# A graph layer on one core: the dense edge counts in rows of nine tiles instead of groups of four

## What is computed

```python
src = h[edge_src]
parts = [relu(h)]
for t in range(3):
    msg = relu(src @ W_e[t].T + b_e[t])
    msg = where((edge_type == t)[:, None], msg, 0)
    parts.append(segment_sum(msg, edge_dst, num_segments=6250))
agg = concatenate(parts, axis=1)                  # 6250 x 512
for t in range(3):
    o = agg @ W_n[t].T + b_n[t]
    updated = where((node_type == t)[:, None], o, updated)
return x + (updated + h)
```

## Time and profile before

| | |
|---|---|
| median of 3 runs | 1460.96 us (1460.74 to 1462.85) |
| the profiled execution | 1458.84 us, its span 1456.6 us |
| PE busy | 1417.5 us (97%) |
| DVE busy | 1086.0 us (75%) |
| POOL busy | 1003.6 us (69%) |
| ACT busy | 565.4 us (39%) |
| mean granted clock of PE | 0.987 of 2.4 GHz |

### The profile page before, as it was taken

How to read it: one execution, slowest core, us unless ns; L and a number is a source line. 1 busy time by engine, 2 the same in 40 slices (tenths; PEclk the granted TensorE clock), 3 DMA queues, 4 the chain that set the end, 5 groups by cost and what they waited for, 6 DMA issues and landing times.

```text
span 1456.6 us, 29052 instructions
## 1 busy us (share of the span) xinstructions
PE 1417.5 (97%) x10079; PEld 1180.2 (81%) x10079; DVE 1086.0 (75%) x3644; ACT 565.4 (39%) x1099; POOL 1003.6 (69%) x1065
## 2 busy tenths in 40 slices
PE   7969999999999999999999999999999999999997
PEld 3447888888888888888888888888888888888874
DVE  5888887877887778878777878777766777677632
ACT  5755444344444334434434434334323333323310
POOL 2347777777777777777777777777777777777760
PEclk9989999999999999999999999999999999999998
DMA  8562322322332262323222322432222222222220
GB/s 280 181 190 73 85 77 71 90 76 65 89 90 78 57 200 69 89 68 88 67 72 75 85 70 75 132 108 57 58 66 63 68 62 61 58 73 62 62 54 25
DMA packets 95629, 126.32 MB, mean 87 GB/s; under 512 B 21135, under 2 KB 72838, under 8 KB 95484
## 3 DMA queue, kind: packets, MB, share of 16 engines
q0 software_dynamic: 32384, 66.39, 18.0%
q1 hardware_dynamic: 62222, 57.05, 12.2%
q10 hardware_dynamic: 878, 1.02, 0.2%
HBM read 98.69 MB, written 25.68 MB: 85 GB/s over the span
## 4 chain that ended last, share of the span: by engine, by line
PE 92%; DVE 4%; issue 1%; DMA 1%; ACT 1%; POOL 0%; DVEq 0%; SPq 0%; ACTq 0%; POOLq 0%
PE ps L684 41%; PE ps L668 25%; PE ps L654 14%; PE ps L703 7%; PE ps L701 3%; PE ps L591 1%; PE ps L700 1%; DMA message_table<-work 1%; PE ps L691 1%; DVE arena L1059 1%; DVE work L1150 0%; DVE lhot L1061 0%; PE ps L589 0%; DMA work<-message_table 0%; DVE acc L1125 0%
## 5 line engine op out<-in xcount | busy, mean ns | idle before, releaser
L531 POOL DMA_INDIRECT rows<-message_table,idx x1012 | 980.1, 968 | 359.6 <-issue 279.0
L829 ACT CAST arena<-ps 128x500 f16<-128x500 f32 x900 | 473.9, 579 | 779.1 <-PE ps L668 768.9
L684 PE MATMUL ps<-mem,arena 128*120 128x384 bf16 x3675 | 681.1, 328 | 1.5 <-DVE mem L1155 1.5
L684 PEld LDWEIGHTS ps<-mem,arena 128*120 128x120 f16 x3675 | 480.2, 135 | 90.1 <-issue 4.4
L1059 DVE TENSOR_SCALAR arena<-iota_j,jkey 128x400 bf16<-128x400 f16 (+2 forms) x1800 | 492.4, 334 | 79.8 <-PE ps L668 77.6
L668 PE MATMUL ps<-arena,lhot 128*128 128x200 bf16 (+2 forms) x3600 | 441.0, 272 | 10.4 <-DVE lhot L1061 6.7
L668 PEld LDWEIGHTS ps<-arena,lhot 128*128 128x128 bf16 x3600 | 353.8, 105 | 56.3 <-DVE lhot L1061 7.9
L1125 DVE TENSOR_TENSOR acc<-ps,acc 128x20 f32 (+1 forms) x703 | 134.2, 191 | 239.8 <-PE ps L654 154.0
L1061 DVE TENSOR_TENSOR lhot<-ps,lkey 128x512 bf16<-128x512 f32 x448 | 303.4, 677 | 0.0
L654 PEld LDWEIGHTS ps<-onehot,rows 128*128 128x128 f32 x2024 | 254.5, 194 | 10.8 <-issue 6.5
L654 PE MATMUL ps<-onehot,rows 128*128 128x27 f32 x2024 | 249.0, 263 | 5.6 <-DVE acc L1125 5.6
(11 more groups left out here) (107 smaller groups left out, 330.5 us busy)
## 6 DMA issues: line engine op xcount, KB each, us to landing
rows<-message_table,idx POOLq DMA_INDIRECT x1012
message_table<-work SPq DMA_DIRECT2D x49, 192.0 KB, 2.0
work<-message_table SPq DMA_DIRECT2D x21, 448.0 KB, 4.4
kept_planes<-work SPq DMA_DIRECT2D x14, 672.0 KB, 3.2
mem<-kept_planes SPq DMA_DIRECT2D x14, 672.0 KB, 4.7
own_hT<-work SPq DMA_DIRECT2D x49, 64.0 KB, 1.7
work<-own_hT SPq DMA_DIRECT2D x49, 64.0 KB
xr<-in_x_dram SPq DMA_DIRECT2D x48, 64.0 KB, 2.1
```

The costliest lines, as they stand in the source:

```text
L531: pool.indirect_dma_start(out=rows[:, g % SLOTS, u, :], out_offset=None, in_=table_rows, in_offset=bass.IndirectOffsetOnAxis(ap=idx[:, g, ...
L684: m = pe.matmul(psQ[q % 2][0:BG * WG, 0:3 * D], counts[q % 2][:, c * MC + e, :], planes[:, c * MC + e, :, :].rearrange("p v d -> p (v d)") ...
L829: act.copy(counts[q % 2][:, half * HH:(half + 1) * HH, k * WG:(k + 1) * WG], psB[m % 3][:, 0:HH * WG].rearrange("p (h w) -> p h w", w=WG)) ...
```

## The change

The last 79,274 edges (79,488 places) are cut into 69 *wide rows* of nine tiles (1152 edges) instead of 150 groups of four. A wide row has 40 slots, with offsets `D_OFF` and widths `D_WID` (sum 72) for its nine tiles; three wide rows make a batch (again 120 columns in a product), 23 batches, 69 with the three types. The gathered groups are 248. There are 49 values of h in place of 50.

A build is now half a wide row: side 0 has the hots of tiles 0 to 4, side 1 of tiles 5 to 8; tile 4 reaches over the middle and has buffers of its own. A build has two parts of ten slots each, all 49 values of h in one bank (490 columns), and a tile that crosses a border of ten slots is multiplied in two pieces: 3, 4, 4 and 3 matmuls for the four parts, 14 a wide row. The column hot is laid out with the slot outside and h inside, and the matmul's output is the same PSUM layout as before (h outside, here ten slots inside) but written in the order of the hot. ACT copies a part of 490 to ten columns of `counts`. One iota serves all widths. The edge list needs 12 loads for 16. DVE's preparation works on two arrays of 512 and one of 1152 per partition. DVE adds three times 40 slots per batch. DVE waits for the last turned keys before the second build's hots, where it waited before the fourth's.

```diff
-BATCHES = 25
-BG = 6
+BATCHES = 23
+BW = 3
+BG = 2 * BW
+WT = 9
+WE = WT * P
...
-LEFT = 12
 WG = 20
-HB = 50
-HH = HB // 2
+D_OFF = (0, 3, 8, 11, 16, 21, 24, 27, 31)
+D_WID = (9, 9, 8, 8, 7, 6, 7, 9, 9)
+D_WS = 9
+D_MID = 21
+D_AT = 5
+MT = 4
+SL = 40
+PC = 10
+OWN = ((0, 1, 2, 3), (5, 6, 7, 8))
+LEFT = 24
+HB = 49
...
+            def hots(i, u):
+                if u == MT:
+                    return lmid[:, i // 2 % 2, :], jmid[:, i // 2 % 2, :]
+                return lhot[:, i % HOTS, OWN[i % 2].index(u), :], jhot[:, i % HOTS, JAT[u]:JAT[u] + HB * D_WID[u]]
+
             def count(i):
                 pe.wait_ge(dhot_ok, i + 1)
-                for half in range(2):
-                    m = 2 * i + half
+                for part in range(2):
+                    m = 2 * i + part
                     if m >= 3:
                         pe.wait_ge(d_count, m - 2)
-                    to = psB[m % 3][:, 0:HH * WG].rearrange("p (h w) -> p h w", w=WG)
-                    for u in range(TPG):
-                        a = JAT[u] + half * HH * WID[u]
-                        t = pe.matmul(to[:, :, OFF[u]:OFF[u] + WID[u]], lhot[:, i % HOTS, u, 0:P],
-                                      jhot[:, i % HOTS, a:a + HH * WID[u]],
-                                      start=(u == 0), stop=(u == TPG - 1), skip_group_check=True)
+                    low = (2 * (i % 2) + part) * PC
+                    tiles = [u for u in range(WT) if D_OFF[u] < low + PC and D_OFF[u] + D_WID[u] > low]
+                    to = psB[m % 3][:, 0:HB * PC].rearrange("p (h w) -> p w h", w=PC)
+                    for u in tiles:
+                        a, z = max(D_OFF[u], low), min(D_OFF[u] + D_WID[u], low + PC)
+                        rows_hot, cols_hot = hots(i, u)
+                        t = pe.matmul(to[:, a - low:z - low, :], rows_hot,
+                                      cols_hot[:, HB * (a - D_OFF[u]):HB * (z - D_OFF[u])],
+                                      start=(u == tiles[0]), stop=(u == tiles[-1]), skip_group_check=True)
                     t.then_inc(d_build, 1)
...
-                    act.copy(counts[q % 2][:, half * HH:(half + 1) * HH, k * WG:(k + 1) * WG],
-                             psB[m % 3][:, 0:HH * WG].rearrange("p (h w) -> p h w", w=WG)).then_inc(d_count, 1)
+                    act.copy(counts[q % 2][:, :, a:a + PC],
+                             psB[m % 3][:, 0:HB * PC].rearrange("p (h w) -> p h w", w=PC)).then_inc(d_count, 1)
...
-                for u in range(TPG):
-                    w = WID[u]
-                    dve.tensor_scalar(jhot[:, i % HOTS, JAT[u]:JAT[u] + HB * w], iota_j[w][:, :],
-                                      float(t * HB * w), jkey[:, g, u:u + 1], ALU.add, ALU.is_equal)
-                dve.tensor_tensor(lhot[:, i % HOTS, :, :], (iota_l[:, :] if i < 2 else iota_n).unsqueeze(1).to_broadcast([P, TPG, P]),
-                                  lkey[:, g, :].unsqueeze(2).to_broadcast([P, TPG, P]), ALU.is_equal).then_inc(dhot_ok, 1)
+
+                def column_hot(to, u):
+                    dve.tensor_scalar(to, iota_j[:, 0:HB * D_WID[u]], float(t * JT), jkey[:, w, u:u + 1],
+                                      ALU.add, ALU.is_equal)
+
+                numbers = iota_l[:, :] if i < 2 else iota_n
+                for u in OWN[side]:
+                    column_hot(jhot[:, i % HOTS, JAT[u]:JAT[u] + HB * D_WID[u]], u)
+                if side == 0:
+                    column_hot(jmid[:, i // 2 % 2, :], MT)
+                    dve.tensor_tensor(lmid[:, i // 2 % 2, :], numbers, lkey[:, w, MT:MT + 1].to_broadcast([P, P]),
+                                      ALU.is_equal)
+                u = OWN[side][0]
+                full = [P, len(OWN[side]), P]
+                dve.tensor_tensor(lhot[:, i % HOTS, :, :], numbers.unsqueeze(1).to_broadcast(full),
+                                  lkey[:, w, u:u + len(OWN[side])].unsqueeze(2).to_broadcast(full),
+                                  ALU.is_equal).then_inc(dhot_ok, 1)
...
+            for u in range(WT):
+                dve.scalar_tensor_tensor(out=tile(e_rel, u), in0=tile(e_dst, u), scalar=float(D_OFF[u]),
+                                         in1=lo[:, SB_:GB].to_broadcast([P, P]), op0=ALU.subtract, op1=ALU.subtract)
...
-                for k in range(BG):
-                    add_to(acc[:, t, at_col(dense_cols[k])], psQ[q % 2][:, 3 * D + k * WG:3 * D + (k + 1) * WG],
-                           ADD_D[q] - BG + k + 1)
+                for k in range(BW):
+                    add_to(acc[:, t, at_col(dense_cols[k], SL)], psQ[q % 2][:, 3 * D + k * SL:3 * D + (k + 1) * SL],
+                           ADD_D[q] - BW + k + 1)
```

More of the change, by code:

```diff
@@ L108, in touches, with wide_touches @@
         return SLOPE * g - SLACK - MID <= (i + 1) * P - 1 and SLOPE * g + AHEAD + WG > i * P
+    def wide_touches(w, i):
+        first = SLOPE * (GD + w * WE / GE)
+        return first - SLACK - D_MID <= (i + 1) * P - 1 and first + AHEAD + SL > i * P
     def plan(hand):
@@ L113, in plan @@
         last = [at[q * MC + MC - 1] for q in range(NQ)]
-        done = list(range(GD)) + [last[NQ - BATCHES + k // BG] + 2 for k in range(ND)]
-        ready = [max(done[g] for g in range(G) if touches(g, i)) for i in range(NB)]
+        wide_done = [last[NQ - BATCHES + w // BW] + 2 for w in range(NW)]
+        ready = [max([g for g in range(GD) if touches(g, i)] + [wide_done[w] for w in range(NW) if wide_touches(w, i)])
+                 for i in range(NB)]
         order = sorted(range(NB), key=lambda i: (ready[i], i))
@@ L196, in build @@
         e_key = prep(mem, 0)
[L197 to L203, removed]
+        e_jlo = mem[:, EW:EW + 2 * WE].rearrange("p (a j) -> p a j", a=2)
+        e_hi = mem[:, EW + 2 * WE:EW + 3 * WE].bitcast(I32)
+        spare = mem[:, EW + 3 * WE:]
+        AB = HB * BW * SL
+        JW = HB * max(sum(D_WID[u] for u in own) for own in OWN)
+        JAT = {u: HB * sum(D_WID[v] for v in own if v < u) for own in OWN for u in own}
         JB = max(AB, NB * D)
@@ L519, in _ @@
                 pool.wait_ge(edge_done, done + 1)
-                for k in range(EW // GE):
-                    a = array * EW + k * GE
-                    pool.memset(flat[:, a:a + GE], 0.0).then_inc(acc_zero, 1)
+                for k in range(4):
+                    a = array * EW + k * EW // 4
+                    pool.memset(flat[:, a:a + EW // 4], 0.0).then_inc(acc_zero, 1)
             pool.wait_ge(turn_a, IDX + SB_)
@@ L564, in weight @@
                 n[0] += 1
-            pe.wait_ge(consts, 8)
+            pe.wait_ge(consts, 6)
             for k in range(WAKE):
-                pe.matmul(psE[k % 2][:, 0:HB * WIDE], iota_l[:, :], iota_j[WIDE][:, :], start=True, stop=True)
+                pe.matmul(psE[k % 2][:, 0:HB * WIDE], iota_l[:, :], iota_j[:, 0:HB * WIDE], start=True, stop=True)
             pe.wait_ge(ident_ok, 1)
@@ L630, in _ @@
                             pe.wait_ge(key_ok, 1)
-                        turn(m, TPG, lambda u: e_key[:, m - KEY, part(u)])
+                        turn(m, TPG, lambda u: near(e_key)[:, m - KEY, part(u)])
                     else:
@@ L1015, in _ @@
             for u in range(TPG):
-                m = dve.scalar_tensor_tensor(out=parts(e_ok, u), in0=parts(e_rel, u), scalar=float(WID[u]),
-                                             in1=parts(e_ok, u), op0=ALU.is_lt, op1=ALU.mult)
+                dve.scalar_tensor_tensor(out=parts(e_ok, u), in0=parts(e_rel, u), scalar=float(WID[u]),
+                                         in1=parts(e_ok, u), op0=ALU.is_lt, op1=ALU.mult)
+            for u in range(WT):
+                m = dve.scalar_tensor_tensor(out=tile(e_ok, u), in0=tile(e_rel, u), scalar=float(D_WID[u]),
+                                             in1=tile(e_ok, u), op0=ALU.is_lt, op1=ALU.mult)
@@ L1116, in _, with at_col @@
             cols = [dve.alloc_register(f"col{k}") for k in range(4)]
-            dense_cols = [dve.alloc_register(f"dense_col{k}") for k in range(8)]
-            def at_col(reg):
-                return bass.ds(dve.snap(reg, min_val=0, max_val=NA - WG), WG)
+            dense_cols = [dve.alloc_register(f"dense_col{k}") for k in range(4)]
+            def at_col(reg, width):
+                return bass.ds(dve.snap(reg, min_val=0, max_val=NA - width), width)
             def add_to(there, sums_, count):
```

198 lines of the change are left out of this document (113 added, 85 removed).

## The result

The changed kernel takes 1654.0 us (median of four runs, 1649.2 to 1655.9) where the kernel before takes 1460.9: 1.132 times as long (95% interval 1.129 to 1.135), slower by 193 us. The profiled execution is one of 1653.8 us with a span of 1652.1.

What follows compares the result with a forecast made beforehand. PE was taken to bound the kernel, busy 97% and 92% of the chain. 1458.8 + 256 (builds) - 48 (products) - 4 (gathered groups) - 3 (turns, tail) - 2 (start) = 1658 us, 1660 at the median; range 1500 to 1830.

Steps and rivals of the forecast that it cites:

- Builds: PE's build matmuls: 450 builds become 207 wide rows at 2.98 us, 617 us against 361, +256 us.
- singles: PSUM elements of a build written without their even-odd neighbour right beside; forecast at 0.42 ns more each, one column's time.
- the average of 0.55: Extra ns per element without its neighbour, from a whole old build: 109 ns over 200 such elements.
- Products: PE's 384-column products: 3675 become 3381, 294 fewer at 0.163 us, -48 us.
- gathered groups: PE's gathered groups: 253 become 248, 5 fewer at 0.81 us, -4 us.
- Start: Edge loads and DVE's preparation before the builds: fewer loads, longer preparation, -2 us (-5.6 to +3).
- Tail: End after the last batch: fewer additions, six finishes behind the last products as before; -3 us together with fewer transposes.
- DVE and ACT: Engines beside PE: DVE about 1075 us, up to 1405 if odd lengths lose pace, ACT about 435; both stay hidden.
- A higher price per single: Build matmuls: unpaired PSUM elements cost more than a column each; 1758 us at 0.55 ns, up to 1962; chance 12%.
- A smaller price: Build matmuls: 0.2 ns per unpaired PSUM element, from start distances; 1502 us; chance 8%.
- A free stride: Build matmuls: the old 109 ns a charge per matmul, not on addresses; faster, 1395 us; chance 13%.
- the branch with no charge at all: Build matmuls: neither addresses nor matmuls charged extra, 1.51 us a wide row; 1354 us in total.

Runs made afterwards that it cites:

- before_odd_starts: Kernel before with all build matmuls 200 columns wide, in runs of 8 from odd slots 1, 3, 9 and 11: 1478.6 us, 1.011 of the kernel before.
- before_pairs: Kernel before with all build matmuls 200 columns wide, in runs of 8 from slots 0, 4, 8 and 12: 1428.4 us, 0.975 of the kernel before.
- before_one_single: Kernel before with build matmuls of 7, 9, 7 and 9 slots from even slots 0, 2, 8 and 10: 1447.5 us, 0.991 of the kernel before.
- changed_again: The changed kernel itself, run again on the chip of the third slots_outside run: 1654.7 us, 1.132 of the kernel before.
- slots_outside: Changed kernel with PSUM laid out slot outside, h inside, ACT turning it while copying: third time 1382.0 us, 0.947 of the kernel before; earlier 1684 and 1676 us.
- before_pairs_even: before_pairs with the second half's hots read from even elements too: 1712 us for 1727, 0.993, on a chip with PE gaps; a build 687 ns.

## Why the prediction was right, point by point

*Builds.* Forecast 2.98 us a wide row, measured 2.89; forecast +256 us for all. Measured are 207 x 2.89 = 599 against 363, and the product behind each of the 414 builds takes 203 ns to the next start for 163 (172 behind the old builds), 17 us against 4: some +249. The mechanism and its size stood: the price from the one matmul of the earlier trace rows whose singles stand side by side was right, 0.42 ns, against the average of 0.55. The 0.09 us too many lie at the borders of a build: its first matmul passes on 42 ns early (329 for 371 with 441 columns, 83 for 125 with 147), and the product behind the last one pays 40 more, so a wide row with the two products behind its builds costs 2.97 us. before_odd_starts has the same in small (11 ns less at the first, 9 more behind the last). That looks like a queue ahead of PSUM which fills at the first and empties at the last; no run here looked into it. The reading of 0.42 had some luck in it: the start distance of the same matmul gave 0.2 ns, and the durations of later ones in before_odd_starts, 282 ns, would have given (282 - 249) / 50 = 0.66.

*Products* -48 and *gathered groups* -4 us: the pace is 163 ns and 0.81 us as before. From the first build to the start of the last product the changed kernel takes 1519.8 us and the kernel before 1321.1, 198.7 more, where builds, products, groups and turns had been summed to 203.

*Start.* Forecast -2, measured +4.8: the first build starts at 92.4 us, not at 87.7. This term missed. Timeline, DVE and SP, of the changed kernel (answering to the earlier trace rows):

```profile
35.48 0.29 SPq L440 DMA_DIRECT2D acc<-in_edge_type_dram  x1
...
41.52 1.23 DVE L1045 SCALAR_TENSOR_TENSOR rows<-acc 128x1024 f32<-128x1024 int32 x1 [14.55 <-DMA acc<-in_edge_type_dram]
...
49.07 1.90 DVE L1066 SCALAR_TENSOR_TENSOR acc<-acc,lo 128x128 f32<-128x128 int32 x9
...
57.33 1.90 DVE L1076 SCALAR_TENSOR_TENSOR acc<-acc 128x128 f32<-128x128 f32 x9
```

The last edge load leaves at 35.5 instead of 31.4, as SP's loop itself ran later, and DVE starts at 41.5. The granted clock between 30 and 60 us was 0.83 for 1.00. Most of it need not be the change: before_pairs, before_odd_starts and before_one_single have the start of the kernel before word for word, and their first builds begin at 96.2, 90.5 and 91.2 us, with clocks from 0.60 to 1.00 in that stretch. With the kernel before they have 91.4 on average; the changed start, in the changed kernel, changed_again and slots_outside the third time, has 92.4, 93.5 and 94.2. The forecast gain of 2 us does not show; whether the change costs something there stays open. The longer preparation came as worked out: 26.6 us from 41.5 to 68.1 for 24.3, +2.3 for +3.

*Tail.* Forecast -2 of the -3, measured -8.0: from the start of the last product to the end 39.8 us for 47.8. The sentence that six finishes lie behind the last products "as before" is the step that failed: it was seven before (steps 245 to 257, every second) and is six now. The chain, the last product pieces and the finishes behind them, changed kernel:

```profile
1607.97 4.58 PE ps L724 x28
1616.58 1.94 PE ps L743 x6
1622.26 3.44 PE ps L743 x6
1629.77 3.10 PE ps L743 x6
1637.19 2.81 PE ps L743 x6
1642.48 1.94 PE ps L743 x6
1646.91 1.95 PE ps L743 x6
```

*DVE and ACT* stayed hidden: DVE is busy for 1096 us for a forecast 1075 (17 of them because the 207 single-tile row hots take 0.28 us each and not 0.2), and the odd lengths keep the pace: 356 ns for 441 columns beside 344 for 392. Start (7 us worse than forecast) and tail (6 better) cancel by luck, so the sum of 1658 against 1654 looks better than its parts.

*The rivals.* A higher price per single: not in the changed kernel, where singles follow each other, 0.417 ns each; but the dearer singles in front of runs in the kernel before are close to what this rival said of them, and are a good part of why the average was 0.55. A smaller price: no, its 0.2 ns was the border of a build, as the first matmul of before_odd_starts shows (96 ns for 107 further in). A free stride: no. slots_outside shows what it would have been: 1.52 us a wide row, the branch with no charge at all, for which 1354 us were worked out, and a total of 1382, with POOL's gathers at 30.6% of its chain. The outcome by "TensorE: Matmul & The Clock Gate" (Trainium skill), Back-to-back issue gap, N/2.4 + 2.5 ns: right within 5 ns for every matmul of slots_outside (186 ns for 441 columns), wrong by a factor of two for the same columns in the changed kernel. "PSUM — Partial Sum Buffer" (Trainium skill), Specifications, with its lines of two fp32 values, has the rule that decides, and the runs give it its size. Its word that any non-contiguous pattern slows matmuls goes too far: the runs of eight slots in before_pairs_even have gaps of twelve between them and take 86 ns, no more than their columns and 3.

## What to carry to other kernels

Before a matmul's output is written in another order than it lies in PSUM, count the elements that are not written as even-odd pairs in a row: each cost about one column's time more here (some two in front of an odd run), so at a step of ten elements, where every element is a single, PE's pace was halved. Let the engine that copies from PSUM do the turning if it has time to spare; here ACT's copy took 573 ns either way, and moving the stride there made a losing change (1.132) into a gain (0.947). And read a matmul's price from distances between starts of neighbours that differ in one thing; the average over a build mixed cheap and dear singles and would have said 0.55.

## What the runs showed of the hardware that was not expected

- Matmul spacing depends on the parity of the moving operand's first element: 86 ns from an even one, 97 to 107 from an odd one, for 200 columns in runs of eight aligned in PSUM. With runs from odd slots it makes no difference (107 and 108).
- A run of nine slots that begins at an odd slot is dearer than one that begins at an even slot, with as many singles: 225 columns take 119 to 121 ns against 108 to 109.
- Reading the moving operand in steps of 98 bytes: 1142 ns a matmul of 441 columns, 962 ns from start to start at either clock, and a granted clock of 0.74 although PE was busy in all of 2600 us.
- Small matmuls have no floor at 85 ns, as I had left open: in slots_outside 98 columns take 43 ns from start to start and 49 columns 27.
- ACT reads PSUM at a step of 49 elements at full pace.
- The table stage varies by 8 us between four kernels with the same code for it: the first build starts at 87.7 to 96.2 us, the last of them with a granted clock of 0.60 between 30 and 60 us, the others with 1.00.
